# A decoder block on one core: row-table fills moved, first weights unit by column halves, transposes for the expert's base rows, 308 key columns, one row maximum moved in the last tiles

## The reference

```python
x = x + hilbert_attention(layernorm(x), Wqkv, Wproj, mapping)   # 32 keys per block of 64 rows, 16 heads of 32
q, (k, v) = layernorm(x) @ Wq, split(ctx @ Wkv)                  # 16 heads of 64
k, v = concat(null_kv, k), concat(null_kv, v)                    # 155 keys
out = softmax(q * scale @ k.T) @ v @ Wout
x = x + layernorm(out) * ln_scale + ln_bias
y = layernorm(x); probs = softmax(y @ Wr + br)                   # 8 experts, the best takes the row
pos = cumsum(one_hot(argmax)) - rows past 512 of an expert are dropped
x = x + gate * (relu(gate * y @ W1[e] + b1[e]) @ W2[e] + b2[e])
```

## Time and profile before

| | us |
|---|---|
| median of 3 executions (1302.13 to 1304.81) | 1303.67 |
| the profiled execution, device time | 1307.84 |
| its span, first to last instruction | 1306.1 |
| PE busy | 1273.7 (98%) |
| DVE busy | 938.5 (72%) |
| ACT busy | 663.0 (51%) |
| DMA: 123.75 MB, mean 95 GB/s | |

### The profile page before, as it was taken

One profiled execution on the slowest core, in us unless ns is written; L12 is line 12 of the kernel. 1 busy time (PEld: TensorE's weight loads), 2 busy tenths in 40 slices (PEclk: granted clock), 3 DMA queues, 4 the chain that ended last, 5 costly groups with the idle time before them and its releaser, 6 DMA issues.

```text
span 1306.1 us, 31630 instructions
## 1 busy us (share of the span) xinstructions
PE 1273.7 (98%) x12332; PEld 1036.4 (79%) x12332; DVE 938.5 (72%) x1903; ACT 663.0 (51%) x1868; POOL 420.6 (32%) x477
## 2 busy tenths in 40 slices
PE   8999899999999999999999999999999999999998
PEld 7987667777777788888888888888888776888886
DVE  6539778888786776777778777777776786665563
ACT  4447433343333655646556555565555663655552
POOL 3213444454532112223231222322211323455453
PEclk9999999999999999999999999999999999999999
DMA  8972142322224201102012021020102103654630
GB/s 265 318 239 65 51 157 81 91 80 86 92 97 140 82 2 49 50 17 95 29 42 82 18 74 50 34 82 21 70 25 90 66 15 128 232 199 171 182 102 23
DMA packets 69233, 123.75 MB, mean 95 GB/s; under 512 B 12313, under 2 KB 20529, under 8 KB 69090
## 3 DMA queue, kind: packets, MB, share of 16 engines
q1 hardware_dynamic: 60770, 98.17, 22.7%
q0 software_dynamic: 8320, 23.62, 5.3%
HBM read 83.19 MB, written 42.07 MB: 96 GB/s over the span
## 4 chain that ended last, share of the span: by engine, by line
PE 82%; DVE 8%; ACT 4%; DMA 3%; issue 2%; SPq 1%; POOL 0%; DVEq 0%; POOLq 0%; ACTq 0%
PE bank L71 19%; PE bank L73 17%; PE bank L72 17%; PE bank L2362 6%; PE bank L2346 6%; PE bank L2385 4%; PE bank L2377 2%; PE bank L1299 2%; PE bank L1269 2%; DMA raw<-in_L_attn_Wqkv_dram 1%; DMA raw<-in_L_xattn_Wkv_dram 1%; PE bank L2425 1%; PE bank L1243 1%; PE bank L2918 1%; PE bank L2436 1%
## 5 line engine op out<-in xcount | busy, mean ns | idle before, releaser
L1648 ACT ACTIVATE b_prob<-bank,b_neg_top 128x155 f32<-128x155 f32 x496 | 186.7, 408 | 120.3 <-DVE b_neg_top L1864 120.3
L1864 DVE TENSOR_REDUCE b_neg_top<-bank 128x6 f32<-128x930 f32 (+1 forms) x93 | 94.3, 1014 | 58.5 <-PE bank L2362 58.5
L71 PE MATMUL bank<-turned_h,big_h 128*128 128x512 f32 x320 | 131.1, 410 | 1.1 <-DVE turned_l L2124 0.8
L73 PE MATMUL bank<-turned_h,big_l 128*128 128x512 f32 x320 | 125.4, 392 | 0.0
L72 PE MATMUL bank<-turned_l,big_h 128*128 128x512 f32 x320 | 124.8, 390 | 0.0
L71 PE MATMUL bank<-b_wo_h,b_ot_h 128*128 128x512 f32 x256 | 111.6, 436 | 1.9 <-ACT b_ws L1681 1.7
L2346 PEld LDWEIGHTS bank<-ident,b_prob 128*128 128x128 f32 x640 | 92.7, 190 | 20.7 <-issue 5.5
L2346 PE MATMUL bank<-ident,b_prob 128*128 128x128 f32 x640 | 104.0, 285 | 2.2 <-DVE b_prob L1875 1.5
L1648 ACT ACTIVATION_READ_ACCUMULATOR b_prob<-bank,b_neg_top 128x1 f32 x496 | 103.9, 209 | 0.0
L73 PE MATMUL bank<-b_wo_h,b_ot_l 128*128 128x512 f32 x256 | 101.1, 395 | 0.0
L72 PE MATMUL bank<-b_wo_l,b_ot_h 128*128 128x512 f32 x256 | 99.9, 390 | 0.0
(11 more groups left out here) (359 smaller groups left out, 3390.0 us busy)
## 6 DMA issues: line engine op xcount, KB each, us to landing
wide<-in_L_ffn_W_dram SPq DMA_DIRECT2D x16, 1024.0 KB, 7.0
slot_rows<-empty_row SPq DMA_DIRECT2D x8, 1032.0 KB, 14.0
a_xr<-in_x_dram SPq DMA_DIRECT2D x32, 256.0 KB, 2.7
x_scratch<-a_xr SPq DMA_DIRECT2D x32, 256.0 KB, 2.1
tiles<-x_scratch SPq DMA_DIRECT2D x32, 256.0 KB, 3.9
rows<-x_scratch SPq DMA_DIRECT2D x32, 256.0 KB, 3.9
out_dram<-rows SPq DMA_DIRECT2D x32, 256.0 KB, 2.0
rows<-slot_rows SPq DMA_DIRECT2D x7, 1032.0 KB, 8.0
```

The source lines that it names most:

```text
L71: pe.matmul(out, lh, rh, start=first, stop=False)
L73: return pe.matmul(out, ll, rh, start=False, stop=last)
L1648: last = act.activation(prob[:, n % 2, j, h:h + 2 * L2 - 1:2], burst_banks(n, b)[:, h, o:o + L2], ACT.Exp, bias=neg_top[:, n % 2, h, j:j + 1],
L1864: dve.tensor_reduce(neg_top[:, n % 2, :, first:end], burst_banks(n, b)[:, :, 0:(end - first) * L2].rearrange("p h (j k) -> p h j k", k=L2) ...
```

## The change

Six edits:

1. The eight fills of `slot_rows` move from `setup` to self-attention's SP list, behind the loads of steps 6, 7, 10, 11, 14, 15, 18 and 19. `empty_row` gets memory of its own, and DVE's wait on the fills goes.
2. Unit 0 of the weights is loaded, rounded and split by halves of its columns (128 of 256, all eight k), and `opening` takes the first half only.
3. The context's last rows lie at 26 * b in place of 32 * b, so a matmul of the key units has 308 moving columns in place of 320.
4. PE does seven matmuls of the identity by itself (128 columns, float32) before the context's transposes, and nine behind them (`warm`).
5. In `closing`, DVE takes the maxima of burst 1 ahead of the residual, statistics and scaling of burst 0, and ACT does that burst's exponentials ahead of a split of the expert's weights.
6. `turn_first` sets `is_transpose`.

```diff
@@ setup
-    CTX_COLS = 2 * P + 32 * B
+    CTX_COLS = 2 * P + REM * B
+    def first_raw(a):
+        return raw[:, 0, :].rearrange("p (k n) -> p k n", k=KC)[:, :, a * P:(a + 1) * P]
         for a in range(2):
-            sp.dma_start(raw[:, 0, 1024 * a:1024 * a + 1024].rearrange("p (k n) -> p k n", k=4),
-                         first[:, 4 * a:4 * a + 4, :]).then_inc(half_loaded if a == 0 else raw_loaded[0], 16)
+            sp.dma_start(first_raw(a), first[:, :, a * P:(a + 1) * P])\
+                .then_inc(half_loaded if a == 0 else raw_loaded[0], 16)
         for u in range(5, NC + 2):
             load(u)
-            for a in range(2 * (u - 5), min(2 * (u - 5) + 2, 8)):
-                prefill(a)
+        def warm(count):
+            for _ in range(count):
+                pe.matmul(bank[3][:, 0:P], ident[:, :], ident[:, :], start=True, stop=True)
         pe.wait_ge(masks, 2)
+        warm(7)
...
             turn(r, lambda k, r=r: ctx_sb[r // 2][0:rows_, (4 * (r % 2) + k) * P:(4 * (r % 2) + k + 1) * P])
+        warm(9)
@@ opening
-            for half, made in ((0, half_high), (1, raw_high)):
-                pe.wait_ge(made, 1)
...
+            pe.wait_ge(half_high, 1)
+            for k in range(KC):
+                pe.matmul(out, w_h[:, k, :], c_h[:, k, :], start=k == 0, stop=False)
+            pe.wait_ge(turned_low, CR)
+            for k in range(KC):
+                pe.matmul(out, w_h[:, k, :], c_l[:, k, :], start=False, stop=False)
+            pe.wait_ge(half_low, 1)
+            for k in range(KC):
+                last = pe.matmul(out, w_l[:, k, :], c_h[:, k, :], start=False, stop=k == KC - 1)
@@ self_attention
+    PREFILLS = (6, 7, 10, 11, 14, 15, 18, 19)
+        def prefill(a):
+            sp.dma_start(slot_tiles[:, 4 * a:4 * a + 4, :],
+                         empty_row[:, :].rearrange("p (a d) -> p a d", a=1).to_broadcast([P, 4, ROW]))\
+                .then_inc(s["prefilled"], 16)
             if tiled(n + 3):
                 load(n + 3)
+            if n in PREFILLS:
+                prefill(PREFILLS.index(n))
-        dve.wait_ge(late["prefilled"], 16 * 8)
@@ cross_attention, ACT closing
+            expo(n + 1, 1)
             expert_split(2 * t)
-            expo(n + 1, 1)
@@ cross_attention, DVE closing
+            top(n + 1, 1)
             add_residual(n - 2)
...
             if t == 2:
                 route_gates(NG - 2)
-            top(n + 1, 1)
@@ turn_first
-                                 start=k == 0, stop=k == G - 1, skip_group_check=True)
+                                 start=k == 0, stop=k == G - 1, is_transpose=True, skip_group_check=True)
```

## The result

| | before | change |
|---|---|---|
| median of four executions each | 1303.81 | 1296.18 |
| lowest to highest | 1302.13 to 1304.81 | 1295.19 to 1298.25 |
| span of the profiled execution | 1306.1 | 1294.6 |

The ratio is 0.9949, with a 95% interval of 0.9935 to 0.9962: 5 to 8.5 us faster. 1297.3 was forecast.

A forecast was written before the change was run, and what follows sets the result against it. TensorE was taken as the bound, 82% of the chain that ended last. Set-up 4.8, closing 1.1 and `turn_first` 0.5 sum to 6.4 us, taking the median from 1303.67 to 1297.3, range 1293.5 to 1301.0.

The forecast's parts named there:

- Set-up: Set-up as a whole: 3.0 us from opening and columns together plus 1.8 from the stalls, 4.8 gained.
- The stalls: Late set-up: moving the fills removes TensorE's stalls of 1.03 and 0.60 us, 1.8 us gained, bounds 1.0 and 2.0.
- The columns: Key units in set-up: 168 more matmuls shrink by 12 columns, 0.9 us gained.
- The opening: Unit 0's first 24 matmuls: start at 12.1, full clock, end at 15.5, 2.2 us gained; bounds 2.9 and a 2.2 loss.
- a cap of 3.05: Set-up, unit 3: VectorE's split ends at 34.30, TensorE starts at 37.35, so at most 3.05 us can be pulled forward.
- Rival C: Opening doesn't gain, as the clock rises during it or the first half's load is late: 1299.5, chance 0.18.
- Closing: Last tiles: earlier maxima gain 1.80 in tile 28, lose 1.1 in 29, gain 0.4 in 30; net 1.1 us.
- Rival E: Last tiles: closing moves the stall whole, tile 29 giving back all that tile 28 gains: 1298.4, chance 0.08.
- some 0.4 of the 1.60: Tile 30: earlier maxima, limited by VectorE's own work, take about 0.4 us off the 1.60 us stall before `values`.
- `turn_first`: Step to the experts: float32 matmuls become single-record transposes, 0.5 us gained, bounds 0 and 0.6.
- rival D: Before the experts: the clock falls at the transposes, costing 1.7 us in the first products: 1299.0, chance 0.09.
- Rival B: Self-attention: fills hold up GpSimd's gathers, at most 1.2 us per fill by the figures, slower at 1306.9, chance 0.07.

The follow-up runs named there:

- e7: The change with unit 0 loaded and split by halves of its rows, as before, warm kept: 1297.46, ratio 0.9961.
- e10: The change with closing's old order, run beside the change on one chip: 1297.47, ratio 0.9961.
- e6: The change with a second closing order, statistics and routing's last part behind the scaling of burst 1: 1298.74, ratio 0.9975.
- e11: The change with a third closing order, the second with tile 30 mended: 1296.54, ratio 0.9957.
- e2: The kernel before with only the fills of the row table moved to self-attention: 1303.83, ratio 0.9968.
- e3: The change without the sixteen warm matmuls: 1304.23, ratio 0.997.
- e1: The kernel before with only the sixteen warm matmuls added: 1306.67, ratio 0.9987.
- e5: The change with the warm matmuls as transposes, 14 and 18 in place of 7 and 9: 1296.89, ratio 0.9966.
- e9: The change itself timed again, beside three other kernels on one chip: 1297.49, ratio 0.9967.
- e12: The change with GpSimd's bias addition over 8 columns in place of 512 in tiles 27 to 31: 1295.51, ratio 0.995.
- e8: The change with the eight fills at the self-attention steps in which GpSimd gathers: 1297.31, ratio 0.9966.
- e4: The change with closing's order as before: 1301.81, ratio 0.9948.
- the first batch: e1 to e4, run on one chip beside the kernel before, whose median there was 1308.04.

## Why the prediction was right, and where not

**Total.** 6.4 us were forecast and 7.6 measured the first time, 4.7 (1302.19 to 1297.49) the second. Range and sign held. By the stages, the change's two profiles have gained 4.5 and 5.2 us in set-up, lost 0.1 and 1.2 in the last tiles and gained 0.56 behind them: 4.9 and 4.6, near the 4.7. What the first 7.6 holds beyond that isn't shown, so it is partly luck that the forecast lies near it: set-up came out right in sum and wrong in make-up, and closing was wrong.

**Set-up, 4.8 forecast, 4.46 in the profile** (5.2 by the starts near 132.8 in e7 to e10, and from 2.9 in e6 to 5.8 in e11). The stalls: 1.8 forecast, 2.3 by e2. The columns: 0.9 forecast, 0.96 by e3 against e2. The opening: 2.2 forecast. It gained more where it happened, 3.4 at unit 0's second half with the columns, because the clock rose in the context's transposes and the nine cost 2.1 us; the start was 10.83 where I had taken 12.1, outside my bounds on the good side. Then 2.05 went to two waits for VectorE's splits of units 1 and 2. This is the step that failed: "What is late next is this split", at unit 3, with a cap of 3.05. I had looked for the cap at one unit only. At unit 2 before's own rows leave less, VectorE's split and TensorE's start:

```profile
23.71 2.29 DVE L461 TENSOR_TENSOR wc_l<-raw,wc_h 128x2048 fp32r<-128x2048 f32 x1 [1.28 <-ACT wc_h L386]
```

```profile
28.64 0.31 PE L71 MATMUL bank<-ct_h,wc_h 128*128 128x320 f32 x1
```

The split ends at 26.00, so 2.64 can be pulled forward there. In the change's profile this split ended at 27.01 and TensorE started at 27.07, 1.57 earlier than in before. In the other profiles with `warm` but e6's it ended between 25.6 and 27.4, also where the code up to there is the same, so how much of the opening's gain arrives differs from one execution to the next.

The price of the smaller pieces, taken as nothing, shows at unit 1. Its load was issued at 8.68 us, in before at 5.5, and its split ended at 18.89, against 18.40 in before and 18.28 in e7. The eight profiles with `warm`, halves by columns and a context in time all wait there, 0.57 to 0.93, and e1 and e7, with halves by rows, wait less than 0.2 there. It isn't shown to reach self-attention: e7 starts it no earlier than six of the others. A smaller misreading: the prediction lets "the first 48-matmul unit" follow the opening, but what follows is unit 0's second half, 24 matmuls.

Nor are the terms additive, as I had them. By e1, warm is worth nothing with the fills in set-up; by e3, 0.85 to 1.5 without them. I had costed the fills by the two stalls that they made, but they also held a reserve of load time: what TensorE gained anywhere in set-up they would have taken. Rival C (the opening doesn't gain) had 0.18. The clock was up before the first product in all eleven profiles with `warm` but e6's; there the rise came with the opening, and the nine added 3.86 us, near its "4.1 us of delay". e5 settles its rule as well: the Trainium skill's sentence on transposes ("TensorE: Matmul & The Clock Gate", Part 4), that full clock doesn't engage for them, does not hold here.

**Closing, 1.1 forecast, nothing measured** (63.25 against 63.17, 64.33 to 65.69 in the other five profiles; e10 beside e9 the same median). Rival E, at 0.08, had the size but not the place. Tile 28 gained 1.97, tile 29 gave back 0.70 as forecast (0.6 to 1.1), tile 30's `values` gained 0.79 (forecast 0.4), and the piece behind it lost 2.14, of which the forecast says nothing: "some 0.4 of the 1.60" stopped at the wait itself. What stands behind is the scaling of burst 2, late because VectorE is full, and fuller by the collision with GpSimd's addition, which the new order moved beside the scaling of burst 1. The Trainium skill has this: by "SBUF — State Buffer", in "SBUF: two separate sides", the port pair that VectorE and GpSimd share is an exclusive lock, held for the whole instruction by the one that starts first, also where a VectorE instruction with two SBUF inputs meets a GpSimd one that reads SBUF. The trace agrees: the addition ran from 1019.10 to 1020.36, the scaling began at 1019.45, and was 0.77 longer than its 1.13; e12, with the addition cut, took it away. However early the scaling begins beside an addition, it ends 0.98 or 0.99 us after that ends (1021.35, 1037.40 and 1055.34 in the change, 1066.33 in before). In before one such case is in the trace, in tile 30, which I had before me and did not weigh.

**`turn_first`, 0.5 forecast, 0.56 measured**, in all eleven profiles that have the edit (4.14 or 4.15 for 4.70). The clock behind it did not fall (the same 4.14 or 4.15 each time), so rival D's place was wrong. But its mechanism, a fall after sparse work, is there 40 us earlier, behind closing's waits.

**Rival B** (fills against gathers) is excluded by e8: no cost even in the steps that gather.

**What is not the change's.** Self-attention took 303.7 to 305.9 us in the profiles of before and e1 to e4, and 297.5 to 299.3 in the rest. In each of the five long ones TensorE pauses in the middle of 64 small matmuls with nothing to wait for, at the same six places, one in most groups of four tiles; TensorE of e4:

```profile
153.93 0.55 PE L1276 MATMUL bank<-wide,a_k_seg 32*32 32x64 f32 x28 [0.40 <-issue]
...
189.81 0.52 PE L1276 MATMUL bank<-wide,a_k_seg 32*32 32x64 f32 x27 [0.43 <-issue]
```

The brackets read some 0.4 us, but the ends before them are modelled late. Against e10, the same kernel without them, the next product comes 0.81 to 0.96 later at each of the six, 5.4 together, which is the 5.26 between the two self-attentions. The nine other profiles have none of the six. It goes with the chip or the hour, and kernels of both kinds have it. The median of before is 5.9 to 6.3 us higher in the first batch than in the other two, so there the ratios should leave it out. In the comparison of the result that isn't shown: before's profile has the pauses and took 4.2 us more than before's median, the change's has none. What makes them stays open.

## What to carry to other kernels

A queue of loads that just keeps pace hides how much it holds: a gain on TensorE ahead of it brings nothing until it is loosened (e1), so such edits are costed together, and the cap is looked for at every unit from the first on, not at one. Taking a wait away in a stretch where VectorE is full moves it; follow VectorE's queue to the second and third consumer behind the one that waited, and look at what GpSimd then runs beside. When two profiles differ by more than the medians, split them by stages and look for the stages that a kernel with identical code there has both ways.

## What was not expected of the hardware

- VectorE's product of two SBUF operands over 930 columns takes 1.13 us, beside GpSimd's 512-column addition 1.39 to 1.90; that over 620 columns 0.81 and, in e6 and e11, 1.79 to 1.80.
- Where the scaling meets the addition it ends 0.98 or 0.99 us after it, wherever it began.
- Transposes raise TensorE's clock as plain matmuls do (e5).
- The clock fell to its lower level after two waits of 0.96 and 1.94 us with some small matmuls between, in five of six profiles with the change's order, and in one of them not; in set-up it fell after one wait of 1.56 us (e6); around cross-attention's first tile it fell in 6 of 14 profiles, whatever the kernel, and cost 1.1 to 1.45 us.
- Pauses of TensorE inside a run of 64 small matmuls, 0.7 to 1.0 us each and six in a whole self-attention, in five profiles, and at none of these places in nine others.
